# Decay sums of a state-space mixer as differences of running sums, formed on VectorE during the MLP

## The chip, the cores and the metric

One core of one Trainium2 chip runs the kernel. The metric is the device time of one execution in microseconds (us). Before the change it is 813.77 us, the median of three runs (813.22 to 813.79). All arithmetic is fp32; each fp32 matrix product shows as two MATMUL records in the trace.

## The reference

Four sequences of 512 tokens with 256 features pass a Mamba-2 style layer with an MLP, and then a mixture of 8 experts of which each token takes 2. Cut to what the change touches (h heads = 8, chunks of 128 tokens, state 128):

```python
dt = softplus(zxbcdt[..., -NHEADS:] + dt_bias)
xBC = silu(dw_causal_conv(xBC, conv_w, conv_b))      # x, B and C
A_cum = cumsum(dA, axis=-1)                          # dA = dt * A, within a chunk
L = exp(segsum(dA))                                  # exp(A_cum[l] - A_cum[s]) for s <= l, else 0
Y_diag = einsum('bcln,bcsn,bhcls,bcshp->bclhp', C, B, L, x * dt)
states = einsum('bcln,bhcl,bclhp->bchpn', B, exp(A_cum[-1] - A_cum), x * dt)
# the state is carried from chunk to chunk; Y_off = C @ state, scaled by exp(A_cum)
y = Y_diag + Y_off + D * x
y = rmsnorm(y * silu(z), mixer_norm_w)
h1 = res + y @ out_proj_w
out = h1 + silu(h2 @ gate_w) * (h2 @ up_w) @ down_w  # h2 = rmsnorm(h1)
```

## The kernel before

Every engine has an instruction list of its own, written out by hand; semaphores join them, and each engine takes its instructions strictly in that order. The list of each engine is a `body(b, prev, nxt)` for one sequence: sequence 0, a loop (two turns) over sequences 1 and 2, and sequence 3. `prev` adds the router's work for the sequence before, `nxt` the projections for the next one. SBUF is one tensor named `big`, PSUM one named `ps` with 8 banks of 512 columns, so rows of the trace name only these two and lines tell operations apart.

A body has two halves. The first is the scan over the four chunks c of 128 tokens. On TensorE: `seg_` (L434) multiplies a triangular matrix by the masked steps, which gives the sums of dA between any two tokens for all 8 heads (128x1024, banks 4 and 5); `front` (L358, L424) transposes x and B and forms the scores C.B; `yT_` transposes the gated y of the chunk before; `back` forms C.state (`off`, L446), the diagonal product of 8 heads (L451) and the chunk's own state (L459); `out_` (L476) is the output projection of the chunk before; `xnT_` and `logits` (L358, L494) are the router's product for the sequence before, one chunk at a time. On GpSimd: `masked_dA` (L1394) makes the masked steps, `scaled_x` (L1399) is x·dt, `plus_x_D` (L1404) adds D·x, `gated` (L1410) multiplies by silu(z), `scale_y` (L1361, L1415, L1417) turns the sum of squares into a scale. On VectorE: `front` (L1041, L1044) masks the scores and multiplies them into the decays, `off` (L1050, L1052), `y_` (L1059, L1062), `state` (L1067, L1071), `h1_` (L1082 to L1090), `decayed_x` (L1078), and `xn_` (L1099), the normalised rows of the sequence before. On ScalarE: `decay` (L787) is the Exp of the sums, then copies out of PSUM, D·x (L807) and the sum of squares of y (L829).

The second half holds dt (L374), the decays' small products (`dec_`, L382), the projections and the convolution of the next sequence (L391, L402, L1026), and the MLP (L547, L552, L566), whose end on TensorE is the end of the body. In it VectorE multiplies gate by up (L1255) and does the router's slots (L1149 to L1159), after which GpSimd scatters them. After the fourth sequence follow the tail of the routing and 39 expert tiles.

## Time and profile before

| | us |
|---|---|
| time, median of 3 runs | 813.77 |
| the profiled execution's own time | 808.96 |
| its span, first to last instruction | 807.1 |
| TensorE busy | 728.0 (90%) |
| VectorE busy | 577.3 (72%) |
| GpSimd busy | 307.4 (38%) |
| ScalarE busy | 227.4 (28%) |

The profiled execution is a single one, and its time lies 4.81 us below the median of the runs. In the rows further down PE is TensorE's matrix products, PEld its weight loads, DVE VectorE, ACT ScalarE, POOL GpSimd and SP the engine that issues the plain DMAs. "L434" is line 434 of the kernel before. The idle time in square brackets is what passed on that engine before the row, with the engine whose instruction ended it. A row of the order of time may hold several instructions of one line; its length is from the first start to the last end, so neighbouring rows overlap a little, and the time from start to start is what one costs the engine.

### The profile page before, as it was taken

Reading aid. Unit: us, or ns where it says so; the run is one execution under the profiler, and the core shown is the slowest. Engines: PE = TensorE matmul, PEld = TensorE weight load, DVE = VectorE, ACT = ScalarE, POOL = GpSimd, SP = SyncE. Lnnn points to the kernel's source line nnn. Section 1 sums busy time; section 2 is a strip of 40 time slices with the busy share of each in tenths; the row PEclk is TensorE's granted clock in tenths of the full one; section 3 lists DMA queues with packets and bytes.
Section 4 is the critical chain, followed back from the end, with each engine's and each line's share of the span. In section 5 each row is a group of like instructions: output and inputs, shape, how many; then the busy total and the mean of one; then the engine's idle time right before and its main releaser. Section 6 shows DMA issues by size and latency. Waiting matters only on the chain.

```text
span 807.1 us, 10348 instructions
## 1 busy us (share of the span) xinstructions
PE 728.0 (90%) x2751; PEld 464.5 (58%) x2752; DVE 577.3 (72%) x1370; ACT 227.4 (28%) x482; POOL 307.4 (38%) x505
## 2 busy tenths in 40 slices
PE   5888999899998999979608999999999999999992
PEld 3466547664667547655504666666666666666661
DVE  4686827868477865853634888888888888888870
ACT  1654544544444534631102111111111111111110
POOL 1266203740456315532242333344433344333422
PEclk9999999999999999999758999999999999999997
DMA  9800001000010000038617211111211112111111
GB/s 324 293 2 1 1 0 53 2 0 0 2 52 0 0 0 27 26 120 274 181 31 276 47 32 26 27 26 29 35 28 26 26 26 32 32 26 26 26 15 19
DMA packets 30167, 43.74 MB, mean 54 GB/s; under 512 B 4099, under 2 KB 23875, under 8 KB 30128
## 3 DMA queue, kind: packets, MB, share of 16 engines
q1 hardware_dynamic: 21600, 33.15, 12.3%
q0 software_dynamic: 8544, 10.30, 8.0%
q8 instruction: 12, 0.20, 0.1%
q14 instruction: 11, 0.09, 0.0%
HBM read 33.84 MB, written 9.75 MB: 54 GB/s over the span
## 4 chain that ended last, share of the span: by engine, by line
PE 64%; DVE 11%; issue 9%; POOL 9%; DMA 3%; ACT 2%; DVEq 0%; POOLq 0%; ACTq 0%; SPq 0%
PE ps L701 28%; PE ps L714 14%; PE ps L391 5%; PE ps L402 3%; PE ps L547 3%; PE ps L358 3%; PE ps L552 3%; POOL lists L1426 2%; POOL big L1404 2%; DVE big L1318 2%; PE ps L476 1%; DVE big L1026 1%; PE ps L566 1%; PE ps L434 1%; PE ps L374 1%
## 5 line engine op out<-in xcount | busy, mean ns | idle before, releaser
L1318 DVE STREAM_TRANSPOSE big<-big 32x224 f32<-32x224 f32 x608 | 244.8, 403 | 9.1
L701 PE MATMUL ps<-big 128*128 x624 | 242.7, 542 | 1.1 <-ACT big L932 1.1
L701 PEld LDWEIGHTS ps<-big 128*128 128x128 f32 x624 | 119.0, 191 | 106.1 <-issue 104.1
L1361 POOL TENSOR_TENSOR big<-big 128x1 f32<-128x1 f32 x179 | 56.6, 316 | 280.3 <-DVE big L1326 159.5
L714 PE MATMUL ps<-big 128*128 x546 | 124.5, 380 | 2.1 <-DVE big L1338 1.3
L714 PEld LDWEIGHTS ps<-big 128*128 128x128 f32 x546 | 100.8, 190 | 15.0 <-issue 2.9
L938 ACT ACTIVATE big<-ps 128x896 f32<-128x896 f32 x39 | 35.8, 917 | 217.2 <-PE ps L701 217.2
L358 PE MATMUL ps<-big 128*128 128x128 f32 (+1 forms) x327 | 52.3, 281 | 39.9 <-DMA big<-lists,big 16.0
L358 PEld LDWEIGHTS ps<-big 128*128 128x128 f32 (+1 forms) x327 | 39.8, 144 | 69.6 <-issue 28.6
L1333 DVE TENSOR_TENSOR big<-big,ps 128x896 f32<-128x896 f32 x39 | 42.4, 1087 | 47.5 <-PE ps L701 47.4
L1503 POOL DMA_INDIRECT out_rows<-big x39 | 63.3, 1623 | 23.8 <-issue 23.8
L1026 DVE SCALAR_TENSOR_TENSOR big<-ps,big 128x511 f32<-128x511 f32 (+2 forms) x72 | 52.9, 746 | 11.0 <-ACT big L778 9.4
L391 PE MATMUL ps<-big 128*128 128x512 f32 x96 | 47.6, 634 | 0.8 <-DVE big L1026 0.8
L932 ACT ACTIVATE big<-ps 128x256 f32<-128x256 f32 x39 | 14.9, 383 | 111.6 <-PE ps L358 111.6
L1426 POOL DMA_INDIRECT lists<-big x32 | 31.9, 997 | 37.9 <-DVE big L1159 28.6
L1492 POOL DMA_INDIRECT big<-xn_rows,big x39 | 40.2, 1030 | 5.9 <-issue 0.5
L566 PE MATMUL ps<-big 128*128 128x256 f32 x192 | 42.1, 379 | 0.0
L566 PEld LDWEIGHTS ps<-big 128*128 128x128 f32 x192 | 36.3, 190 | 5.2 <-issue 0.5
L547 PE MATMUL ps<-big 128*128 128x512 f32 x80 | 37.9, 596 | 1.0 <-DVE big L1245 1.0
L552 PE MATMUL ps<-big 128*128 128x512 f32 x80 | 37.6, 592 | 0.0
L451 PEld LDWEIGHTS ps<-big 128*128 128x128 f32 x256 | 31.4, 195 | 8.3 <-issue 6.3
L1399 POOL TENSOR_TENSOR big<-big 128x512 f32<-128x512 f32 x16 | 17.5, 1092 | 48.6 <-ACT big L795 48.6
(173 smaller groups left out, 924.4 us busy)
## 6 DMA issues: line engine op xcount, KB each, us to landing
big<-in_w SPq DMA_DIRECT2D x24, 896.0 KB, 11.8
out_rows<-big SPq DMA_DIRECT2D x4, 512.0 KB
xn_rows<-big SPq DMA_DIRECT2D x4, 512.0 KB
big<-in_hidden SPq DMA_DIRECT2D x1, 1536.0 KB, 11.8
big<-in_in_proj SPq DMA_DIRECT2D x1, 1288.0 KB, 6.9
big<-in_gate SPq DMA_DIRECT2D x1, 640.0 KB, 12.8
big<-in_up SPq DMA_DIRECT2D x1, 640.0 KB, 8.7
big<-in_down SPq DMA_DIRECT2D x1, 640.0 KB, 9.2
```

The lines of the kernel that those rows point to most:

```text
L358: return nc.tensor.transpose(out_ap, in_ap, ident[0:n, 0:n])
L391: last = mm(bank(4 + j % 2), win[:, k, INNER + j * P:INNER + (j + 1) * P], hT[:, k, :], start=(k == 0), stop=(k == KD - 1))
L547: last = mm(bank(bk), wgate[:, k, j * P:(j + 1) * P], h2T[:, k, :], start=(k == 0), stop=(k == KD - 1))
L552: last = mm(bank(bk + 1), wup[:, k, j * P:(j + 1) * P], h2T[:, k, :], start=(k == 0), stop=(k == KD - 1))
L566: last = mm(bank(t % 2)[:, 0:D], hid[:, j, t * P:(t + 1) * P], wdown[:, j, :], start=(j == 0), stop=(j == JB - 1))
L701: last = mm(bank(bk + n)[:, 0:HALF], xT[:, k, :], expert_cols(e, off + k * M + n * HALF, HALF), start=(k == 0), stop=(k == KD - 1))
L714: last = mm(bank(7)[:, 0:D], hTs[:, half, j * P:(j + 1) * P], expert_cols(e, 2 * KD * M + j * D, D), start=(j == 0), stop=(j == MB - 1))
L1026: last = V.scalar_tensor_tensor(xc[:, j, s:SEQ], bank(4 + j % 2)[:, 0:SEQ - s], vec[:, w:w + 1], xc[:, j, s:SEQ], ALU.mult, ALU.add)
L1318: last = V.transpose(hTs[c * SQ:(c + 1) * SQ, half, :].rearrange("p (j t) -> p j t", j=MB)[:, :, q * SQ:(q + 1) * SQ], ha[q * SQ:(q + 1) * ...
L1361: G.tensor_tensor(idle[:, k:k + 1], half[:, 0:1], half[:, 0:1], ALU.add)
L1426: G.indirect_dma_start(lists, bass.IndirectOffsetOnAxis(ap=slots[:, t, k:k + 1], axis=0), recs[:, t, k, :], None).then_inc(rec_out, 16)
L1503: G.indirect_dma_start(out, bass.IndirectOffsetOnAxis(ap=sidx, axis=0), ys, None, compute_op=ALU.add, bounds_check=TOKENS + P - 1, oob_is_ ...
```

## The change

The sums between two tokens are no longer a product on TensorE. `dec_` makes one more small product, the running sums of dA with the 32 pairs of chunk and head as rows; ScalarE copies it to SBUF (`cumT`), SyncE writes it to HBM (16 KB) and reads it back four times, each time 4 KB spread to all 128 partitions (`spread`), straight into `em`, which now has four chunks instead of two. VectorE subtracts the running sum of the row's own token and takes the minimum with 0 (`apart`, eight instructions of 128x128 for one chunk), ScalarE forms Exp in place (`decay`), VectorE multiplies by the masked scores (`scores`). For a next sequence all of this stands in the MLP: `apart` behind the first four gate-up products, `decay` behind the last gate activation, `scores` between the additions of the MLP's output. The first sequence has `apart` among its convolutions and the last three `scores` in its scan.

The transposes of B and the scores C.B of all chunks are formed at once during the MLP (`bg_`, banks 4 and 5) and masked in one instruction (`masked_G`). `decayed_x` moves from VectorE to GpSimd. The gate is distributed: GpSimd multiplies (off + D·x) by silu(z), VectorE multiplies the diagonal product out of PSUM by silu(z) (`yz`) and adds both. The transposed y has bank 5 instead of sharing bank 0 with the output projection. The router's transposes and logits are done in two halves of two chunks instead of four. `masked_dA` and `seg_` are gone.

```diff
+            def spread(n):
+
+
+                sp.wait_ge(cumT_taken, nth(n, 1, 0))
+                if not (isinstance(n, int) and n == 0):
+                    sp.wait_ge(y_ps, n * CH)
+                sp.dma_start(cum_rows, cumT[0:CH * HEADS, :]).then_inc(cum_out, 16)
+                sp.wait_ge(cum_out, nth(n, 16, 15))
+                for c in range(CH):
+                    sp.dma_start(em[:, c, :].unsqueeze(1),
+                                 cum_rows[c * HEADS:(c + 1) * HEADS, :].rearrange("(o h) l -> o (h l)", o=1).unsqueeze(0).to_broadcast([P, 1, HEADS * P])).then_inc(cum_in[c], 16)
...
+                if nxt:
+                    spread(b + 1)
...
+                mm(bank(1)[0:CH * HEADS, P:2 * P], dA.rearrange("p a b -> p (a b)"), tri_upto, start=True, stop=True).then_inc(dec_ps, 1)
...
-            seg_(0, 0, False)
+            bg_(0)
             front(0, 0, False)
 
             def body(b, prev, nxt):
                 for c in range(CH):
-                    if c + 1 < CH:
-                        seg_(b, c + 1, prev)
-                    if prev and c > 0:
-                        logits(b - 1, c - 1, b)
                     if c + 1 < CH:
                         front(b, c + 1, prev)
                     if c > 0:
                         yT_(b, c - 1)
-                    if prev and c > 0:
-                        xnT_(b - 1, c, b)
+                    if prev and c == 1:
+                        xnT_(b - 1, 0)
                     back(b, c, prev)
-                    if prev and c == 0:
-                        xnT_(b - 1, c, b)
+                    if prev and c == 2:
+                        logits(b - 1, 0)
+                        xnT_(b - 1, 1)
                     if c > 0:
                         out_(b, c - 1)
-                if prev:
-                    logits(b - 1, CH - 1, b)
+                    if prev and c == 3:
+                        logits(b - 1, 1)
                 if prev:
                     pe.wait_ge(lg_taken, b)
                 if nxt:
-                    pe.wait_ge(bg_taken, nth(b, CH, CH - 1))
+                    pe.wait_ge(xs_taken, nth(b, CH, CH - 1))
                     hT_(b + 1)
                 yT_(b, CH - 1)
                 if nxt:
                     pe.wait_ge(s_taken, nth(b, CH - 1, CH - 2))
                     dt_(b + 1)
-                    pe.wait_ge(seg_taken, nth(b, CH, CH - 1))
                     xbc_(b + 1, 0)
                 out_(b, CH - 1)
                 if nxt:
...
+                    if nxt and j == 1:
+                        bg_(b + 1)
                     if prev and j == 1:
                         positions(b - 1)
-                    if nxt and j == JB - 2:
-                        seg_(b + 1, 0, True)
...
+                A(cumT[0:CH * HEADS, :], bank(1)[0:CH * HEADS, P:2 * P], ACT.Copy).then_inc(cumT_taken, 1)
+                A(cums.rearrange("p a b -> p (a b)"), bank(1)[:, CH * HEADS:2 * CH * HEADS], ACT.Copy).then_inc(cums_taken, 1)
                 A(dec.rearrange("p a b c -> p (a b c)"), bank(1)[:, 0:3 * CH * HEADS], ACT.Exp).then_inc(dec_taken, 1)
...
             def decay(b, c):
-                act.wait_ge(seg_ps, nth(b, CH, c))
-                A(em[:, c % 2, :], bank(4, 2), ACT.Exp).then_inc(seg_taken, 1)
+                act.wait_ge(apart_ready, nth(b, CH, c))
+                A(em[:, c, :], em[:, c, :], ACT.Exp).then_inc(decays, 1)
...
-                        decay(b, c + 1)
                         front(b, c + 1)
                     if c >= 1:
                         yT_copy(b, c - 1)
-                    if prev:
-                        xnT_copy(b - 1, c)
+                    if prev and c in (1, 2):
+                        xnT_copy(b - 1, c - 1)
                     if c >= 1:
                         square_y(b, c - 1)
...
-                    if nxt and j == JB - 2:
-                        decay(b + 1, 0)
-                if nxt:
+                    if nxt and j == 2:
+                        bt_copy(b + 1)
+                if nxt:
+                    decay(b + 1, 0)
                     front(b + 1, 0)
+                    for c in range(1, CH):
+                        decay(b + 1, c)
...
+            def apart(n, c):
+
+
+                v.wait_ge(cums_taken, nth(n, 1, 0))
+                v.wait_ge(cum_in[c], nth(n, 16, 15))
+                for hh in range(HEADS):
+                    q = slice(hh * P, (hh + 1) * P)
+                    last = V.tensor_scalar(em[:, c, q], em[:, c, q], cums[:, c, hh:hh + 1], 0.0, ALU.subtract, ALU.min)
+                last.then_inc(apart_ready, 1)
+
+            def masked_G(n):
+                v.wait_ge(bg_ps, nth(n, 1, 0))
+                V.tensor_tensor(gm, bank(5).rearrange("p (c l) -> p c l", c=CH),
+                                tri_upto.unsqueeze(1).to_broadcast([P, CH, P]), ALU.mult).then_inc(gm_ready, 1)
+
+            def scores(b, c):
+                v.wait_ge(gm_ready, nth(b, 1, 0))
+                v.wait_ge(decays, nth(b, CH, c))
+                V.tensor_tensor(heads(em[:, c, :]), heads(em[:, c, :]),
+                                gm[:, c, :].unsqueeze(1).to_broadcast([P, HEADS, P]), ALU.mult).then_inc(em_ready, 1)
...
                 v.wait_ge(y_ps, nth(b, CH, c))
                 if c == 0:
-                    v.wait_ge(xsd_ready, nth(b, CH, c))
-                    V.tensor_tensor(yb[:, 0, :], xsd[:, 0, :], bank(6), ALU.add).then_inc(y_taken, 1)
-                else:
-                    v.wait_ge(y3_ready, nth(b, CH - 1, c - 1))
-                    V.tensor_tensor(yb[:, c % 2, :], yb[:, c % 2, :], bank(6), ALU.add).then_inc(y_taken, 1)
+                    v.wait_ge(z_taken, nth(b, CH, CH - 1))
+                if not (isinstance(b, int) and b == 0 and c == 0):
+                    v.wait_ge(y4_ready, b * CH + c)
+                V.tensor_tensor(yz, bank(6), sz[:, c, :], ALU.mult).then_inc(y_taken, 1)
+                v.wait_ge(y_taken, nth(b, CH, c))
+                v.wait_ge(y3_ready, nth(b, CH, c))
+                V.tensor_tensor(yb[:, c % 2, :], yb[:, c % 2, :], yz, ALU.add).then_inc(y4_ready, 1)
...
             def body(b, prev, nxt):
 
                 V.tensor_copy(cur_mv, mv)
                 V.tensor_copy(cur_rs, rs).then_inc(cur_kept, 1)
                 v.wait_ge(cur_kept, nth(b, 1, 0))
-                if prev:
-                    xn_(b - 1)
                 for c in range(CH):
-                    if c + 1 < CH:
-                        front(b, c + 1)
+                    if not prev and c + 1 < CH:
+                        scores(b, c + 1)
...
@@ -1216,8 +1245,8 @@
                     state(b, c)
                     if c > 0:
                         h1_(b, c - 1)
-                    if c + 1 < CH - 1:
-                        decayed_x(b, c + 1)
+                    if prev and c == 0:
+                        xn_(b - 1)
                     if nxt and c == 0:
                         ln1_stats(b + 1)
...
+                    if nxt and j < CH:
+                        apart(b + 1, j)
+                    if nxt and j == 2:
+                        masked_G(b + 1)
+                if nxt:
                     for t in range(CH):
+                        scores(b + 1, t)
                         add_mlp(b, t)
-                        if t == 1:
-                            decayed_x(b + 1, 0)
                     ln2_stats(b, ALL, CH)
...
-            def masked_dA(n, c):
-                g.wait_ge(dA_ready, nth(n, 1, 0))
-
-                if not (isinstance(n, int) and n == 0 and c < 2):
-                    g.wait_ge(seg_ps, n * CH + c - 1)
-                G.tensor_tensor(heads(mda[:, c % 2, :]), tri_upto.unsqueeze(1).to_broadcast([P, HEADS, P]),
-                                over_head(dA[:, c, :], P), ALU.mult).then_inc(mda_ready, 1)
...
             def gated(b, c):
-                g.wait_ge(y_taken, nth(b, CH, c))
                 if c == 0:
+                    g.wait_ge(xsd_ready, nth(b, CH, c))
                     g.wait_ge(z_taken, nth(b, CH, CH - 1))
-                G.tensor_tensor(yb[:, c % 2, :], yb[:, c % 2, :], sz[:, c, :], ALU.mult).then_inc(y4_ready, 1)
+                    G.tensor_tensor(yb[:, 0, :], xsd[:, 0, :], sz[:, 0, :], ALU.mult).then_inc(y3_ready, 1)
+                else:
+                    g.wait_ge(y2_ready, nth(b, CH - 1, c - 1))
+                    G.tensor_tensor(yb[:, c % 2, :], yb[:, c % 2, :], sz[:, c, :], ALU.mult).then_inc(y3_ready, 1)
...
-                    if c + 2 < CH:
-                        masked_dA(b, c + 2)
+                    if c == 0:
+                        gated(b, 0)
                     if c + 1 < CH:
                         scaled_x(b, c + 1)
+                    if c + 1 < CH - 1:
+                        decayed_x(b, c + 1)
                     if c > 0:
+                        scale_y(b, c - 1)
                         plus_x_D(b, c)
-                        scale_y(b, c - 1)
-                    gated(b, c)
+                        gated(b, c)
...
-                if nxt:
-                    masked_dA(b + 1, 0)
-                    masked_dA(b + 1, 1)
                 if prev:
                     scatter(b - 1)
                 if nxt:
                     scaled_x(b + 1, 0)
+                    decayed_x(b + 1, 0)
...
```

TensorE, chunk 2 of the loop's scan (line 358 are transposes, 446 to 459 the back of the chunk, 494 the logits, 476 the output projection of chunk 1), before:

```order
L428 REGISTER_ALU
L434 MATMUL ps<-big 128x512 x2
L491 REGISTER_ALU
L494 MATMUL ps<-big 128x8 x2
L358 MATMUL ps<-big 128x128 x5
L424 MATMUL ps<-big 128x128
L358 MATMUL ps<-big 128x128 x6
L446 MATMUL ps<-big 128x512
L451 MATMUL ps<-big 128x64 x8
L456 REGISTER_ALU
L459 MATMUL ps<-big 128x512
L476 MATMUL ps<-big 128x256 x4
```

and after (379 transposes, 460 to 475 the back, 510 logits, 492 output projection):

```order
L379 MATMUL ps<-big 128x128 x8
L460 MATMUL ps<-big 128x512
L465 MATMUL ps<-big 128x64 x8
L470 REGISTER_ALU
L475 MATMUL ps<-big 128x512
L506 ISA
L510 MATMUL ps<-big 128x8 x4
L379 MATMUL ps<-big 128x128 x4
L492 MATMUL ps<-big 128x256 x4
```

The product L434 is gone from the top, front's transposes and those of y follow each other directly (x8), and the router's transposes stand as four (L379 x4) behind the logits, which themselves stand behind the back of the chunk. Before, the router's two transposes stood ahead of the back, among the six.

On ScalarE the Exp and one copy of each chunk are gone; in chunk 2 the copy of the transposed xn (`xnT_copy`) keeps its place between the copy of the transposed y and the square of y.

GpSimd, chunk 2 of the same scan up to the gate (1399 scaled_x, 1404 plus_x_D, 1361 to 1417 scale_y, 1410 the gate), before:

```order
L1399 TENSOR_TENSOR big<-big 128x512
L1403 REGISTER_ALU
L1404 TENSOR_TENSOR big<-big 128x512
L1361 TENSOR_TENSOR big<-big 128x1
L1415 TENSOR_SCALAR big<-big 128x1
L1416 REGISTER_ALU
L1417 TENSOR_TENSOR big<-big 128x1
L1410 TENSOR_TENSOR big<-big 128x512
```

and after (1422 scaled_x, 1392 to 1450 scale_y, 1434 plus_x_D, 1443 the gate):

```order
L1422 TENSOR_TENSOR big<-big 128x512
L1392 TENSOR_TENSOR big<-big 128x1
L1448 TENSOR_SCALAR big<-big 128x1
L1449 REGISTER_ALU
L1450 TENSOR_TENSOR big<-big 128x1
L1433 REGISTER_ALU
L1434 TENSOR_TENSOR big<-big 128x512
L1443 TENSOR_TENSOR big<-big 128x512
```

scale_y of the chunk before now stands ahead of plus_x_D.

## Rows read from the trace of the kernel before

**Rows 1.** Stretch, its length, busy us of each engine (instructions), granted clock, DMA share, GB/s.

```profile
...
131.00:224.00 93.00, 87.86 (x368) 56.67 (x367) 64.50 (x158) 43.26 (x100) 40.88 (x47) 0.98 0.04 12
...
```

**Rows 2.** TensorE in order of time, loop turn 1: start, us, what, [idle before].

```profile
...
130.95 1.88 PE L434 MATMUL ps<-big 128*128 128x512 f32 x4
132.66 0.71 PE L358 MATMUL ps<-big 128*128 128x128 f32 x5
...
137.54 0.44 PE L358 MATMUL ps<-big 128*128 128x128 f32 x2 [1.29 <-DVE big L1099]
...
151.87 1.02 PE L446 MATMUL ps<-big 128*128 128x512 f32 x2
152.73 1.89 PE L451 MATMUL ps<-big 128*128 128x64 f32 x16
154.46 1.08 PE L459 MATMUL ps<-big 128*128 128x512 f32 x2
155.38 1.89 PE L476 MATMUL ps<-big 128*128 128x256 f32 x8
...
159.39 1.46 PE L358 MATMUL ps<-big 128*128 128x128 f32 x6 [1.78 <-DVE big L1087]
...
169.02 1.92 PE L374 MATMUL ps<-big 128*128 128x8 f32 x16 [0.50 <-DVE big L992]
...
176.04 0.75 PE L382 MATMUL ps<-big 128*128 128x32 f32 x6
...
213.48 10.53 PE L566 MATMUL ps<-big 128*128 128x256 f32 x48
...
```

**Rows 3.** The same for TensorE in the first and the last sequence.

```profile
...
76.92 1.92 PE L374 MATMUL ps<-big 128*128 128x8 f32 x16 [0.38 <-DVE big L992]
...
316.76 1.88 PE L434 MATMUL ps<-big 128*128 128x512 f32 x4
...
345.27 0.84 PE L358 MATMUL ps<-big 128*128 128x128 f32 x6 [2.21 <-DVE big L1087]
...
351.56 0.63 PE L358 MATMUL ps<-big 128*128 128x128 f32 x4 [0.72 <-POOL big L1410]
...
```

**Rows 4.** Groups by line, 131 to 169 us: busy us, mean ns of one, idle before.

```profile
...
L1410 POOL TENSOR_TENSOR big<-big 128x512 f32<-128x512 f32 x4 | 5.1, 1270 | 3.0 <-PE ps L434 3.0
L1404 POOL TENSOR_TENSOR big<-big 128x512 f32<-128x512 f32 x3 | 4.6, 1542 | 5.4 <-DVE big L1050 5.4
...
L1099 DVE TENSOR_SCALAR big<-big 128x256 f32 x4 | 3.4, 897 | 1.2 <-POOL big L1471 1.2
...
L1399 POOL TENSOR_TENSOR big<-big 128x512 f32<-128x512 f32 x3 | 3.2, 1054 | 0.0
...
L1050 DVE TENSOR_TENSOR big<-ps,big 128x512 f32<-128x512 f32 x3 | 2.1, 685 | 1.0 <-PE ps L446 1.0
...
L829 ACT ACTIVATE big<-big 128x512 f32<-128x512 f32 x3 | 1.9, 636 | 0.0
L1417 POOL TENSOR_TENSOR big<-big 128x1 f32<-128x1 f32 x3 | 1.8, 589 | 0.2
...
```

**Rows 5.** VectorE in order of time, first, third and last sequence.

```profile
...
42.42 2.80 DVE L1044 TENSOR_TENSOR big<-big 128x1024 f32<-128x1024 f32 x1
...
199.22 1.28 DVE L1255 TENSOR_TENSOR big<-big,ps 128x512 f32<-128x512 f32 x2
...
203.22 0.16 DVE L1149 TENSOR_TENSOR big<-ps,big 128x8 f32<-128x8 f32 x1
...
205.55 0.17 DVE L1159 CAST big<-big 128x8 int32<-128x8 f32 x1 [0.16 <-DVE big L1158]
...
357.65 1.14 DVE L1239 TENSOR_SCALAR big<-big 128x256 f32<-128x256 f32 x4 [1.75 <-POOL big L1461]
...
```

**Rows 6.** DMA issues of the page: count, size, us from issue to landing.

```profile
...
big<-in_hidden SPq DMA_DIRECT2D x1, 512.0 KB, 3.4
...
```

**Rows 7.** Stretches of 1.5 us in turn 2, columns as in rows 1.

```profile
...
262.00:263.50 1.50, 1.50 (x4) 0.98 (x5) 0.77 (x4) 0.69 (x3) 0.00 (x0) 0.50 0.00 0
263.50:265.00 1.50, 1.50 (x3) 0.47 (x3) 1.29 (x7) 0.28 (x2) 0.98 (x3) 0.50 0.00 0
...
```

149 lines of the change are left out of this document (74 added, 75 removed).

## The prediction

> **What bounds the kernel now.** I read the busy time by stretch first, then the order of time on TensorE through one sequence, then the groups by line for the price of one instruction, and last the other engines where TensorE waits. From 131 to 224 us, one turn of the loop over sequences, TensorE is busy 87.9 of 93.0 us, VectorE 64.5, GpSimd 40.9, ScalarE 43.3 [rows 1]. Behind the four sequences lies the expert part, which the change leaves alone. So each sequence is bounded by TensorE, except for short idle stretches in the scan over four chunks. I count times within a turn from S, the end of the previous MLP: 130.95 and 316.76 us [rows 2, 3]. The idle stretches end with VectorE's normalised rows (137.54) and with an h1 row (159.39) [rows 2]. The scan ends, for the rest of the sequence, when the dt product starts: S+38.07 (169.02) [rows 2]; in the first sequence at 76.92; in the last one the transposes of y for chunk 3 start at 351.56, S+34.8 [rows 3].
>
> **Removed from TensorE.** The product of the masked steps, L434: 132.66 - 130.95 = 1.71 us [rows 2], four per sequence, sixteen in all: 27.4 us. Added are a product of 32 by 128 (about 0.2 us beside the three of L382) and nothing else; the transposes of B and the scores C.B move from the four chunks into the MLP, 4 x 0.33 = 1.3 us. Three of the four L434 lie in the scan and one in the MLP. If TensorE stayed the bound, the whole 27.4 us less four times 0.2 would be won. It can only be won where nothing else is then late, so I followed the scan again with the durations of the rows.
>
> **The MLP stretch.** VectorE takes on, behind each of the first four gate-up products, eight TENSOR_SCALAR of 128x128, and once the mask (0.6). The trace has no such instruction of 128 columns. Nearest row: L1239, four of 256 columns with one per-partition scalar, 1.14 us, so (1.14 - 0.41)/3 = 0.24 us from start to start [rows 5]; half the columns can't cost more, and no less than half of it, 0.12. Near to neither end, I take the middle: 0.18, 1.45 us for eight. VectorE then runs, from the first hid product at 199.22: five hid products of 0.61, 2.5 for the routing slots (203.22 to 205.72), 0.6, four times 1.45 [rows 5]: it ends at about 211.5. TensorE's first down product, at 213.48 before [rows 2], would be due at 213.48 - 1.71 - 0.33 + 1.3 = 212.7. So it fits with 1.2 us to spare at 0.18, and ends 0.9 us late at 0.24. The Trainium skill ("VectorE: DVE Perf Modes", Mode 2×_2P) says that an fp32 tensor_scalar within SBUF takes two elements a cycle; the row agrees as far as it goes (256 columns in 0.24 us), and by the page alone the sum would be the same. ScalarE's Exp of the decays moves behind the last gate activation, its multiplications by G between the additions of the MLP's output; the down products (10.5 us from 213.48) hide both. The transfers: dec is at 176.04 [rows 2], the spread tiles are first read at 199.8, behind the first hid product. A 512 KB transfer took 3.4 us to land [rows 6]; a write of 16 KB and four of 512 KB would land 6 to 16 us after 177, so 0 on the path; even at double that only the first tile would be near. Gain of the MLP stretch with the missing L434 (1.71), less the 1.3 moved in, plus 0.33 that front no longer has, less 0.2: 0.5 us in each of three sequences.
>
> **The scan, sequences 1 and 2.** Prices: a GpSimd product of 128x512 1.25 (L1410), the first kind 1.05 (L1399), a VectorE one from PSUM 0.6 to the next and 0.69 to its end (L1050), GpSimd's three small ones of scale_y 1.1 with the power of 0.59 (L1417), ScalarE's square 0.64 (L829) and 0.2 to read its sum [rows 4].
> Chunk 0: GpSimd's power for the rows of the sequence before ends at S+2.8 as now, then it gates x·D (to 4.1). VectorE adds yz behind it, but its add has both inputs in SBUF and meets GpSimd's next product. In the trace such a product took 2.80 instead of 1.22 us with GpSimd at work [rows 5], and the four normalised rows 0.9 each instead of 0.35 [rows 4]; so I let each wait for GpSimd's end: add until 5.7, state copy 6.3, the four rows of xn, now behind them, until 8.7. TensorE, done with chunk 0 at S+3.5, transposes y at 5.8, then waits for xn until 8.8: chunk 1's off product starts at about S+9.3, before at S+11.07. The Trainium skill ("SBUF — State Buffer", Who interferes with whom) has the same as an exclusive lock of one port pair; the 2.80 us row agrees.
> Chunk 1: ScalarE copies the transposed xn first and has the sum of squares at 10.8; GpSimd's scale_y now stands ahead of plus_x_D: 12.0, 13.2, and gating 14.5; VectorE adds to 15.3, state 15.9; off(2) at S+16.0. Before S+20.9 (151.87). TensorE had 0.86 + 1.73 + 0.92 + 1.72 of work [rows 2], so 0.45 us idle only.
> Chunk 2: here a new wait stands. ScalarE's copy of the second half of xnT comes ahead of the square of y(1), and TensorE makes that half only behind all of back(2) and the logits: 16.0 + 3.5 + 0.75 + 0.45 = 20.7. So the copy ends at 21.4, the square at 22.2; GpSimd 1.1 + 1.25 + 1.25 to 25.9; VectorE's add 26.7. TensorE finishes out(1) at 22.4 and idles 4.3 us; off(3) at S+27.4. Before S+29.7.
> Chunk 3: VectorE has h1(1), h of the next sequence, off(3) until 30.5; GpSimd 31.9 and 33.1; add 33.9; then h1(2) 1.3 and hT1 0.75: dt at S+36.1 against 38.07. Gain 2.0. What went missing: 5.1 us of L434 and 4 us of idle time were to be had, and the chain y(c) to off(c+1) by way of VectorE, GpSimd twice, VectorE (6 to 6.5 us) and the detour in chunk 2 took the rest. The chain is longer than before by the gate product, since the state is now behind the add that waits for it.
>
> **Sequence 0** has no xn, but GpSimd's decays and ScalarE's Exp of the fourth tile stand ahead of x·D: first product of y at about 44 (45.2 before, where VectorE's product ended [rows 5]), off(1) at 52 to 53, dt 76.6 against 76.92: 0.3. **Sequence 3**: no work for a next one; y(3) is transposed at S+33.2 against 34.8: 1.6.
>
> **The sum.** 0.3 + 2 x 2.0 + 1.6 in the scans, 3 x 0.5 in the MLPs: 7.4 us. Against it stands TensorE's clock. At 159.39, behind 1.78 us idle, six transposes took 1.46 us, at 345.27, behind 2.21 us idle, the same six 0.84 [rows 2, 3]. From 262 to 265 us TensorE was granted 0.50, the level of 1.2 GHz [rows 7]; such a stretch of 3 us costs half of itself, 1.5 us, where TensorE is the bound. The change makes idle stretches of 4.3 us. I take one more such stretch, with what is left of it at its edges 1.7 us, in the whole kernel. 5.7 us remain. The profiled execution took 808.96 us (span 807.1), which is 4.8 below the median of 813.77; the difference is made within the execution and taken off the median: 808.1 us.
>
> **Rivals.**
> A. TensorE stays the bound: the collisions and the detour of chunk 2 cost little, for instance since ScalarE's order matters less than I think. For it: TensorE busy 94% of a turn. Against it: orders fixed in the code, above all the copy ahead of the square. With 4.3 us back in three sequences and half of the other losses it is 813.8 - 5.7 - 13 - 3 = 792; all of it, 787. Chance 0.08.
> B. Half of it: VectorE and GpSimd don't block each other in chunk 0 and 1 (1.0 to 1.5 us each) as I let them. L1099 may have run partly between GpSimd's products. 808.1 - 3 x 2.3 = 801. Chance 0.17.
> C. Slower by the clock: each of the three later sequences idles at S+4, S+7 and S+23. If in all four sequences two stretches at 1.2 GHz fall into work that bounds (hT, dt and xbc behind the scan), that is 8 x 1.5 = 12 us against the two stretches, 3 us, of now: 9 more on the 7.4 gained, 815.4; with the eight at 0.24 us each (0.9 in two sequences) 817.2. It decides from five such stretches more than before. The Trainium skill ("TensorE: Matmul & The Clock Gate", What's actually happening) has the clock throttled by default and released by activity; the trace shows both, a drop after 1.8 us and none after 2.2. Chance 0.13.
> D. No change to be measured: seven collisions of 1 us more than I counted. 813.8. Chance 0.09.
> The forecast as it stands: 0.53, with its own range of 804 to 812.
>
> **How the numbers follow.** A measurement of this kernel tells 0.2% from no change, 1.6 us: faster is below 812.1, slower above 815.4. Faster: A, B and nearly all of the forecast's 0.53, 0.77; same: D, a part of C and the forecast's edge, 0.12; slower 0.11. The range of 8 in 10 leaves out A and the upper part of C: 799 to 815.
>
> **What would show it.** Right: no L434; TensorE idle about 4 us ahead of the y transposes of chunk 3 with a release that leads back to GpSimd and ScalarE's square; xn as releaser at S+8.8; dt at S+36; no wait in the MLP; the spread landed by 195. Wrong: turns of under 88 us (A), an idle TensorE ahead of the first down product (the eight dearer than 0.22 us each), or the granted clock under 0.96 in all turns (C).

## The result, and the profile after

The changed kernel took 835.76 us (median of 4; 828.51 to 838.68) against 813.78 (813.22 to 814.22) for the kernel before, run beside it: a ratio of 1.0246, 95% interval 1.0213 to 1.028. It is slower by 22 us, where 5.7 us less was forecast. The profiled execution took 838.68 us with a span of 836.9. Its page, busy time and the granted clock in 40 slices:

```profile
span 836.9 us, 10346 instructions
...
PE 742.4 (89%) x2695; PEld 482.3 (58%) x2696; DVE 584.1 (70%) x1490; ACT 219.2 (26%) x466; POOL 292.6 (35%) x501
...
PEclk9957999779998799789965999999999999999997
```

TensorE has 56 instructions fewer than before (2751) and yet 14.4 us more busy time (728.0 before). Work has got dearer by the clock: the last line falls to 5, 7 or 8 in slices 3 and 4, 8 and 9, 13 and 14, 17 and 18, once per scan. (The 6 and 5 in slices 21 and 22, behind the routing's tail, have their like in the kernel before, whose line reads 7, 5, 8 in slices 20 to 22.)

TensorE in order of time through one turn of the loop (start, us, what, [idle before]); the turn's S is 140.22:

```profile
140.22 0.60 PE L379 MATMUL ps<-big 128*128 128x128 f32 x4
140.90 2.00 PE L465 MATMUL ps<-big 128*128 128x64 f32 x16
...
145.90 0.65 PE L379 MATMUL ps<-big 128*128 128x128 f32 x4 [1.65 <-DVE big L1095]
149.44 1.12 PE L379 MATMUL ps<-big 128*128 128x128 f32 x4 [2.89 <-DVE big L1125]
150.35 1.91 PE L460 MATMUL ps<-big 128*128 128x512 f32 x2
152.06 3.51 PE L465 MATMUL ps<-big 128*128 128x64 f32 x16
...
171.34 0.66 PE L379 MATMUL ps<-big 128*128 128x128 f32 x4 [4.11 <-DVE big L1095]
172.02 1.71 PE L460 MATMUL ps<-big 128*128 128x512 f32 x2
173.52 3.52 PE L465 MATMUL ps<-big 128*128 128x64 f32 x16
176.83 3.12 PE L492 MATMUL ps<-big 128*128 128x256 f32 x8
...
183.13 1.92 PE L395 MATMUL ps<-big 128*128 128x8 f32 x16 [0.50 <-DVE big L1010]
```

The three waits are those of the prediction: 1.65 us for y(0), xn as releaser (L1125) ahead of chunk 1, and 4.11 us ahead of the transposes of y for chunk 3. What stands behind them isn't: the sixteen products of y take 3.51 us instead of 1.89 [rows 2], the output product 3.12 instead of 1.89. The dt product starts at S+42.9, against S+38.07 before [rows 2] and S+36.1 forecast. In windows (columns as in rows 1) the two stretches behind the waits, and the worst one, in the first sequence:

```profile
148.00:158.00 10.00, 8.56 (x26) 6.35 (x27) 6.50 (x17) 3.11 (x11) 6.34 (x10) 0.52 0.16 54
172.00:179.00 7.00, 6.98 (x23) 5.73 (x24) 4.71 (x11) 1.60 (x5) 4.07 (x7) 0.53 0.00 0
...
42.00:63.00 21.00, 17.93 (x65) 13.03 (x64) 16.63 (x40) 13.83 (x36) 13.66 (x13) 0.52 0.32 116
```

A granted clock of 0.50 is the 1.2 GHz level. Up to 390 us such stretches add up to some 100 us here and to some 13 before.

These two profiled executions lie on opposite sides of their kernels. The one of the kernel before has a granted clock of 0.965 and 808.96 us, where its other executions on record have 0.952 to 0.967 and 811 to 820 us; the one of the changed kernel is the slowest of its four. Their spans differ by 29.8 us, the medians by 22. A second trace of the kernel before, with only its loop written out (e9 below, 817.74 us), has some 30 us at the low level up to 390 us instead of 13. So the turns below overstate what the change cost, 29.8 us where the medians give 22; against e9 the clock added 6 us in a turn instead of 8.

To weigh clock against waits I cut every kernel from one first product of y to the next, a whole turn. In that window the busy time less the length times (1 - clock) is the work at the full clock; the product itself is what the clock added (a little too much, as idle time is counted in). The clock has two digits, so a term is good to half a us. The same turn, before and after:

```profile
133.43:226.33 92.90, 87.76 (x368) 56.57 (x367) 64.51 (x158) 43.26 (x101) 40.88 (x48) 0.98 0.04 11
...
45.28:133.43 88.15, 84.14 (x338) 53.23 (x339) 57.43 (x120) 40.21 (x91) 29.58 (x37) 0.98 0.01 4
```

```profile
140.90:240.14 99.24, 89.19 (x353) 59.26 (x353) 67.70 (x189) 40.90 (x96) 37.35 (x46) 0.90 0.09 33
...
46.62:140.90 94.28, 90.32 (x324) 58.98 (x324) 63.10 (x150) 41.96 (x101) 30.04 (x37) 0.84 0.08 30
```

Before: 85.9 work, 1.9 clock, 5.1 idle. After: 79.3 work, 9.9 clock, 10.05 idle. So 6.6 us of work went, as the four L434 say; 4.9 us of waits came, as I had counted; and 8 us of clock came, which I had not. In the first sequence (the second line of each pair) the turn is 6.1 us longer with no more idle time than before (3.96 against 4.01 us): 7.1 us less work and 13.3 us of clock, 0.84 where it was 0.98. The four sequences give 6.1, 6.3, 6.0 and, with everything behind the last, 10 us, and the start 1.3: together the 29.8 us between the two spans. The expert tiles have no part in it: from their first transposes (451.74 us here, 421.69 before) to the end they take 385.2 and 385.4 us.

In the table of the experiments, three of e1's ten executions and two of e16's nine lay over 1.5% above the fastest of their kernel, the profiled ones among them; their medians and ratios are of the others, and their turns aren't given.

One more thing stands in the second turn of the loop. VectorE, first instruction behind the jump back:

```profile
241.00 0.17 DVE L1204 TENSOR_SCALAR big<-big 128x4 f32<-128x4 f32 x1
245.65 1.02 DVE L1233 COPY big<-big 128x8 f32<-128x8 f32 x1 [4.48 <-issue]
```

It waits for no other engine, only for its own issue, and TensorE then waits 5.03 us for VectorE's add, where the turn before has 1.65. That I had not seen coming. Not all of the 3.4 us more is lost, since xn is then ready sooner (0.78 us of waiting instead of 2.89): the off product of chunk 1 starts at S+12.3 instead of S+10.1. The same copy behind the jump in the kernel before:

```profile
225.91 0.17 DVE L1202 COPY big<-big 128x8 f32<-128x8 f32 x1 [0.36 <-issue]
```

### The profile page after: what moved, and what is told of

It is laid out like the page before. It is cut to its first block, busy times and chain, and to the rows that moved or that the text cites. A ratio compares the mean times of both kernels' runs of the same rounds, so it can differ in the third digit from the quotient of the medians.

```text
span 836.9 us, 10346 instructions
## 1 busy us (share of the span) xinstructions
PE 742.4 (89%) x2695; PEld 482.3 (58%) x2696; DVE 584.1 (70%) x1490; ACT 219.2 (26%) x466; POOL 292.6 (35%) x501
## 4 chain that ended last, share of the span: by engine, by line
PE 72%; issue 10%; DVE 8%; POOL 4%; DMA 3%; ACT 2%; DVEq 0%; POOLq 0%; SPq 0%
PE ps L710 27%; PE ps L723 13%; PE ps L412 5%; PE ps L492 4%; PE ps L379 4%; PE ps L465 3%; PE ps L563 3%; PE ps L568 3%; PE ps L582 2%; PE ps L423 2%; PE ps L460 2%; DVE big L1349 1%; PE ps L395 1%; DVE big L1125 1%; DMA lists<-big 1%
## 5 line engine op out<-in xcount | busy, mean ns | idle before, releaser
L710 PEld LDWEIGHTS ps<-big 128*128 128x128 f32 x624 | 119.1, 191 | 105.9 <-issue 104.0
L379 PE MATMUL ps<-big 128*128 128x128 f32 (+1 forms) x327 | 59.1, 301 | 57.4 <-DVE big L1095 23.6
L723 PEld LDWEIGHTS ps<-big 128*128 128x128 f32 x546 | 100.8, 190 | 14.9 <-issue 2.9
L379 PEld LDWEIGHTS ps<-big 128*128 128x128 f32 (+1 forms) x327 | 44.3, 155 | 88.1 <-issue 26.8
L465 PEld LDWEIGHTS ps<-big 128*128 128x128 f32 x256 | 45.2, 266 | 13.0 <-issue 11.2
L412 PE MATMUL ps<-big 128*128 128x512 f32 x96 | 49.0, 649 | 0.4 <-DVE big L1044 0.4
L1422 POOL TENSOR_TENSOR big<-big 128x512 f32<-128x512 f32 x16 | 19.2, 1201 | 77.2 <-ACT big L806 77.1
L465 PE MATMUL ps<-big 128*128 128x64 f32 x256 | 44.3, 348 | 1.9 <-DVE big L1191 1.1
L492 PE MATMUL ps<-big 128*128 128x256 f32 x128 | 42.0, 486 | 0.7 <-ACT big L830 0.7
L582 PE MATMUL ps<-big 128*128 128x256 f32 x192 | 42.1, 379 | 0.0
L492 PEld LDWEIGHTS ps<-big 128*128 128x128 f32 x128 | 32.6, 261 | 13.3 <-issue 7.0
## 6 DMA issues: line engine op xcount, KB each, us to landing
big<-in_gate SPq DMA_DIRECT2D x1, 640.0 KB, 13.3
```

Source lines behind the costliest of these rows:

```text
L379: return nc.tensor.transpose(out_ap, in_ap, ident[0:n, 0:n])
L412: last = mm(bank(4 + j % 2), win[:, k, INNER + j * P:INNER + (j + 1) * P], hT[:, k, :], start=(k == 0), stop=(k == KD - 1))
L465: last = mm(bank(6)[:, hh * HD:(hh + 1) * HD], em[:, c, hh * P:(hh + 1) * P], xdt[:, c % 2, hh * HD:(hh + 1) * HD], start=True, stop=True)
L492: last = mm(bank(0)[:, 0:D], yTs[:, k, :], wout[:, k, :], start=(k == 0), stop=(k == 3))
L582: last = mm(bank(t % 2)[:, 0:D], hid[:, j, t * P:(t + 1) * P], wdown[:, j, :], start=(j == 0), stop=(j == JB - 1))
L710: last = mm(bank(bk + n)[:, 0:HALF], xT[:, k, :], expert_cols(e, off + k * M + n * HALF, HALF), start=(k == 0), stop=(k == KD - 1))
```

## The experiments

The theory: TensorE lost work that lay between the waits of the scan, so that these waits, which come as forecast, let the clock fall, and the work behind each wait ran at half the clock. Rivals: the waits alone carry the loss; or the jump does. Ratios are to the kernel before, run beside each group. "Turn" is the turn of the loop as above, in the profiled execution; "w / c / i" its work, clock and idle us. Only the first of the loop's two turns is given; the second can differ by several us (changed 98.92, e2 98.93, e5 102.02, e7 90.69, e12 89.0). A fill is one product of `keep_warm(bank, n)`, which both kernels have: n products of the identity with 128x256 constants, which nobody reads.

| kernel | median us | ratio (95%) | turn | w / c / i |
|---|---|---|---|---|
| changed | 835.76 | 1.0246 (1.0213-1.028) | 99.24 | 79.3 / 9.9 / 10.1 |
| e1_square_first | 812.34 | 0.9946 (0.9914-0.9979) | | |
| e2_fill_seg | 825.95 | 1.0104 (1.0075-1.0133) | 93.77 | 83.9 / 4.7 / 5.2 |
| e3_no_seg | 811.7 | 0.9936 (0.9912-0.9959) | 93.07 | 79.2 / 6.5 / 7.4 |
| e4_router_later | 809.29 | 0.9912 (0.9877-0.9947) | 89.39 | 79.0 / 3.6 / 6.9 |
| e5_fill_waits | 831.31 | 1.0153 (1.0116-1.019) | 96.20 | 87.0 / 3.8 / 5.3 |
| e6_unrolled | 833.97 | 1.0213 (1.0175-1.0251) | 94.58 | 79.9 / 4.7 / 9.9 |
| e7_later_fill | 804.4 | 0.9841 (0.9811-0.9871) | 87.11 | 85.9 / 0 / 1.3 |
| e8_later_fill_unrolled | 797.05 | 0.9764 (0.9732-0.9795) | 87.02 | 85.8 / 0 / 1.2 |
| e9_before_unrolled | 817.21 | 1.0004 (0.9983-1.0025) | 94.37 | 85.6 / 3.8 / 5.0 |
| e10_later_unrolled | 808.23 | 0.9903 (0.9868-0.9937) | 89.52 | 79.2 / 3.6 / 6.7 |
| e11_stats_later_fill | 794.12 | 0.9719 (0.969-0.9747) | 85.67 | 84.8 / 0 / 0.9 |
| e12_stats_later | 805.28 | 0.9857 (0.9813-0.9902) | 87.19 | 80.0 / 1.7 / 5.4 |
| e13_before_fill | 818.46 | 1.0038 (1.0019-1.0058) | 92.95 | 90.1 / 0 / 2.8 |
| e14_after_fill_unrolled | 825.27 | 1.0132 (1.0097-1.0166) | 96.08 | 87.0 / 3.8 / 5.2 |
| e15_no_seg_fill | 819.13 | 1.0049 (1.0027-1.0071) | 93.98 | 85.8 / 3.8 / 4.5 |
| e16_no_seg_fit | 809.33 | 0.9931 (0.9902-0.9961) | | |
| e17_after_fit_unrolled | 814.2 | 1.0012 (0.9989-1.0034) | 93.41 | 87.8 / 1.9 / 3.7 |
| e18_stats_later_fit | 795.74 | 0.9765 (0.9736-0.9794) | 87.19 | 83.5 / 1.7 / 2.0 |

**Work taken away, work put in.** Two edits of opposite sense. In the kernel before, the decay sums' product alone is cut to 8 columns (the decays are then not computed):

```
-                for i in range(2):
-                    last = mm(bank(4 + i), tri_after, mda[:, c % 2, i * 512:(i + 1) * 512], start=True, stop=True)
-                last.then_inc(seg_ps, 1)
+                mm(bank(4)[:, 0:8], tri_after, mda[:, c % 2, 0:8], start=True, stop=True).then_inc(seg_ps, 1)
```

> The kernel before with the product L434 cut to 8 columns; so the decays are not computed, everything else and every wait stays. Saves up to 16 x 1.6 = 26 us of TensorE. Clock theory: thinner work alone lowers the granted clock in the scan below that of before; 800 to 812. Wait theory: TensorE was the bound, so 790 to 797, with the granted clock at 0.96.

It was 0.6% faster, 5 us, for 26 us of work taken out. Its turn is no shorter than before (92.90 us there, 94.37 in e9):

```profile
134.80:227.87 93.07, 85.68 (x360) 58.03 (x359) 64.64 (x159) 43.42 (x101) 40.75 (x47) 0.93 0.04 12
```

6.7 us of work went; 2.3 us of idle time and 4.6 of clock took its place. The granted clock, mean of the executions, is 0.936 against 0.957 for the kernel before beside it. The 811.7 us lie at the edge of the clock theory's 800 to 812 and far from the waits' 790 to 797. The new transfers can't be what lowers the clock either: this kernel has none of them. But less work and longer waits came together here, so the run doesn't tell which of the two lowers it. In the changed kernel, useless products were put where L434 had stood, ahead of each chunk of the scan:

```
                 for c in range(CH):
                     if c + 1 < CH:
+                        keep_warm(3, 4)
+                    if c + 1 < CH:
                         front(b, c + 1, prev)
```

> The changed kernel with useless products of TensorE in the places of the removed ones in the scan: four of 128x256 (1.7 us at full clock, the length of L434) at the head of chunks 0 to 2, twelve times in all, into a bank that nobody reads. Clock theory: 20.6 us of work are added and yet the time falls or stays, 815 to 832, since the stretches at 1.2 GHz get shorter or go. Wait theory: the fillers lie in front of work that bounds, or in idle time at best: 836 to 850.

20.6 us of work more made it 10 us faster than the changed kernel, within the expected range. If waits were all, fills could at best be free.

**The order around the waits.** ScalarE's square of y ahead of its copy of xnT:

```
-                    if prev and c in (1, 2):
-                        xnT_copy(b - 1, c - 1)
                     if c >= 1:
                         square_y(b, c - 1)
+                    if prev and c in (1, 2):
+                        xnT_copy(b - 1, c - 1)
```

> The changed kernel (835.8 us), with ScalarE's copy of the transposed xn behind the square of y instead of ahead of it in chunks 1 and 2. The idle stretch of 4.1 us ahead of y's transposes in chunk 3 should go from three sequences. Clock theory (the waits let TensorE's granted clock fall for 7 to 10 us, and that is where the loss lies): 836 - 12 of idle time - some 7 of half-speed work = about 817, with the stretch at 1.2 GHz behind chunk 3's start gone. Wait theory (the waits themselves are the loss, the clock comes along): 836 - 12 = 824 and the granted clock where it was, 0.92.

Two lines give 3% back, some 24 us, more than either expectation. The detour of chunk 2 was real. It had cost waits of 4.11 us in three sequences, 12.3 us, so about as much again came back otherwise, and the granted clock rose from 0.917 to 0.925 in the changed kernel's executions to 0.925 to 0.936 here. Executions of this one program also part by the clock: at 0.936 and 0.933 they took 807.93 and 807.45 us, at 0.926 and 0.925 818.07 and 815.27. Next, TensorE's transposes of xn behind the products of chunk 1, too:

```
-                    if prev and c == 1:
-                        xnT_(b - 1, 0)
                     back(b, c, prev)
+                    if prev and c == 1:
+                        xnT_(b - 1, 0)
```

> The changed kernel with the router's first transposes behind the back of chunk 1 instead of ahead of it, and ScalarE's copies of them behind the square of y. Takes both long idle stretches away (2.9 us in chunk 1 on xn, 4.1 in chunk 3), 21 us in three sequences. Clock theory: also the stretches at 1.2 GHz behind them, 836 - 21 - 15 = about 800. Wait theory: 836 - 21 = 815.

809.29 us lies between what the two theories expected (about 800 and 815). The turn fell to 89.39 us; the first sequence, which has no router part, kept its low stretch from 41 to 61 us.

**Useless work in the waits.** Here I first made two mistakes, which the expectations carry: one 128x256 fill is two instructions and takes 0.43 to 0.47 us, not 0.24; and in e5 and e14 six stood ahead of y(1), where that order has no wait, with two ahead of y(2), where it waits 4.11 us.

```
+            keep_warm(3, 5)
             bg_(0)
@@
                     if c > 0:
+                        keep_warm(3, (4, 6, 2)[c - 1])
                         yT_(b, c - 1)
                     if prev and c == 1:
+                        keep_warm(3, 4)
                         xnT_(b - 1, 0)
@@
+                    keep_warm(1, 3)
                     dt_(b + 1)
```

> The changed kernel with useless 128x256 matmuls of the identity (0.24 us each at the full clock, 0.43 to 0.47 at half) put only where TensorE waits anyway: 5 ahead of the first sequence's C.B products, 4 ahead of the turning of y(0), 4 ahead of xn's transposes, 6 ahead of the turning of y(1), 2 ahead of that of y(2), 3 ahead of the dt product. About 5 us of new work per sequence, against waits of 1.65, 2.89, 4.11 and 1.4 us in the second sequence of the changed kernel. Theory 1 (the clock carries most of the loss: some 100 us of the layer part lie in stretches at 0.50, and work inside those is paid twice): the stretches at 0.50 shrink to under 50 us, the time falls by 12 to 20 us, to 816 to 824. Rival (the waits carry the loss and the low clock is only what they look like): the fills hide in waits or lengthen them, 836 to 842, and the waits keep their places.

It gained some 7 us, half of what was expected, and lies between the ranges of both theories. In the turn shown 7.7 us of fills bought 4.7 of idle time and 6.1 of clock; the second turn got 3.1 us longer, and of the rest the first sequence gave most: its turn took 89.45 us instead of 94.28. The same fills in the order of e4 (there y(1) does wait 2.9 us, and xn no longer does, so its four are left out):

> The version with the router's transposes behind the attention-like product and ScalarE's square ahead of its copy (809.3 us in the last runs), with the same useless matmuls (without the 4 ahead of xn's transposes, which no longer wait). Its stretches at 0.50 are some 78 us up to 392 us. Theory 1: the 20 us at half clock in the first sequence (41 to 62) and two thirds of the others go, time 796 to 803, under both kernels. Rival (waits): 809 to 813.

0.7% faster, 804 us, just above the expected range. With the loop written out as well:

```
-            with eng.Fori(1, SEQS - 1) as b:
+            for b in range(1, SEQS - 1):
                 body(b, True, True)
```

> The version of the run before this one with the loop over the middle sequences written out: if the jump is what holds VectorE up for 5.97 us and TensorE for 6.25 us at 238.36, it takes another 4 to 6 us off, 791 to 799; if not, the two are the same within 1 us.

797.05 us, within the expected 791 to 799. The turn, with a clock of 1.00:

```profile
133.38:220.40 87.02, 85.84 (x382) 58.07 (x382) 67.40 (x189) 40.93 (x96) 37.09 (x45) 1.00 0.11 37
```

e10 is the same without fills, the fourth corner of the square:

> Router's transposes later and the loop written out, without any useless matmuls. With the three runs e4_router_later, e7_later_fill and e8_later_fill_unrolled this makes a square of two edits. Theory (the fills give 5 us or more wherever TensorE waits, whether or not the loop is written out): this takes about 5 us off e4, ratio 0.984 to 0.988, which is 6 to 9 us above e8's ratio of 0.976. Rival (with the jump's stall gone the fills are worth nothing): ratio 0.975 to 0.978.

```profile
135.46:224.98 89.52, 82.78 (x353) 54.27 (x353) 67.48 (x189) 40.81 (x96) 37.13 (x45) 0.96 0.11 36
```

The fills' 6.6 us took 5.5 of idle time and 3.6 of clock; over the kernel 11 us were won by adding some 30 instructions a turn that compute nothing, more than the 6 to 9 expected. (The ratio of e10 itself, 0.9903, lies above both expected ranges: the loop alone gave next to nothing.) The rest of the square shows how the two edits need each other: written out alone the loop brought 0.1% (within the intervals), with fills 0.8%.

The controls. The kernel before, with fills in its own waits (0 to 4 at each), computes the same products:

```
                 if c > 0:
                     pe.wait_ge(o_taken, nth(b, CH, c - 1))
+                if c in (1, 2):
+                    keep_warm(0, (2, 4)[c - 1])
                 pe.wait_ge(y4_ready, nth(b, CH, c))
```

> The kernel before with useless 128x256 matmuls where it waits: 4 ahead of the first sequence's first decay sums, 4 ahead of its first y product (waits of 1.59 and 1.77 us there), and in each sequence 3 ahead of xn's first transposes (1.29), 2 and 4 ahead of the turning of y(1) and y(2) (0.89, 1.78). Clock theory: only some 13 us of its layer part lie at 0.50, so there is little to win: ratio 0.993 to 1.001. Rival (the fills act on something that both kernels have, so they explain nothing of the change): ratio under 0.99, as in the changed kernel's variants (0.9903 to 0.9764 there).

A little slower, outside the expected range on the upper side. The granted clock, mean of the executions, rose only from 0.957 to 0.963: with little time at the low level there is little to win, and the fills cost more than that. And fills in the same places, some more of them, for the kernel without the decay sums' products:

> As e3_no_seg (the kernel before, decay sums' products cut to 8 columns, so the decays aren't computed; ratio 0.9936) with useless matmuls in the waits: 4 ahead of the first decay sums, 5 ahead of the first y product of the first sequence, and in each sequence 6 ahead of xn's first transposes (2.84 us wait), 4 and 4 ahead of the turning of y(1) and y(2) (1.57, 1.78). Of the 26 us removed some 3.3 us per sequence are work again, but inside waits. Clock theory: the 61 us at 0.50 of e3 shrink to under 25, and the time falls by 8 to 14 us, ratio 0.976 to 0.984. Rival (the removal was worth only 4 us because the waits took its place, the clock is a side effect): ratio 0.992 to 0.998.

This failed: 1.0049 where 0.976 to 0.984 was expected. The clock did come back (0.936 to 0.958, mean of the executions), but 6.6 us of fills bought 2.9 of idle time and 2.7 of clock, since those ahead of y stand behind the wait for o_taken and so outlast what is left of the wait. Cut to 6, 1 and 1 (same edit, with 3 ahead of the first sums, and 4 ahead of the first y product, not 5 as the expectation says):

> As e15_no_seg_fill (decay sums' products cut to 8 columns, so the decays aren't computed), with fills cut to what fits in the waits: 3 ahead of the first sums, 5 ahead of the first y product of the first sequence, 6 ahead of xn (2.6 us in a wait of 2.84), 1 and 1 ahead of the turning of y(1) and y(2) (0.43 us each; 4 each before). e15's turn of 93.98 us was 85.7 us of work at the full clock, 3.8 of clock and 4.45 idle. Clock theory: idle 4.5 stays or rises to 5.5, fills fall from 6.6 to 3.5 us, the clock stays at 0.96 or better: turn of 90.5 to 92, ratio 0.980 to 0.990. Rival (a low clock costs nothing that the waits don't cost): as e3_no_seg, turn 92.5 to 93.5, ratio 0.992 to 0.996.

0.9931, the same as without fills, so the rival's number, though the clock did come back here too (0.936 in e3, 0.957 here, mean of the executions). In this kernel the fills cost what the clock gave. A part of it is their place: in e15's second turn those ahead of y(1) stand behind 2.27 us of another wait, on the path. The rest isn't explained, and e15 and e16 leave open what the removal alone would be worth at the full clock. Fills of the right size and place in the changed kernel's own order, loop written out, are the cleanest case; first the order with all its mis-placed fills:

> The changed kernel, order as it was, with the fills of e5_fill_waits and the loop written out. Alone they gave ratios of 1.0153 and 1.0213 against the changed kernel's 1.0246. Theory (clock, and the stall of 4.5 to 5.6 us at the jump, which with its low stretch behind it undid what the fills had won): together more than the sum of both, ratio 0.995 to 1.005. Rival (the waits for xn and y(1), 2.89 and 4.11 us, are themselves the loss): about the sum of both, ratio 1.010 to 1.015.

1.0132: about the sum of both edits, again the rival's number. Against this kernel:

```
-                        keep_warm(3, (4, 6, 2)[c - 1])
+                        keep_warm(3, (3, 0, 8)[c - 1])
@@
-                        keep_warm(3, 4)
+                        keep_warm(3, 6)
                         xnT_(b - 1, 0)
@@
-                    keep_warm(1, 3)
+                    keep_warm(1, 1)
```

> The changed kernel in its own order, loop written out, with fills in the waits it has and of their size: 3 ahead of the turning of y(0) (1.3 us, wait 1.61), 6 ahead of xn (2.6, wait 2.89), none ahead of y(1), 8 ahead of y(2) (3.5, wait 4.12), 1 ahead of dt. e6_unrolled's second turn was 79.9 us of work at the full clock, 4.7 of clock and 9.9 idle: 94.6. Clock theory: the fills take 7.8 us of the 9.9 idle and the 4.7 of clock go: turn of 90 to 91.5, ratio 0.998 to 1.006. Rival (waits alone): 94 to 95, ratio 1.015 to 1.022.

1.0012, in the expected range, against 1.0213 for e6 with the same order, the same waits and no fills: 16 us for nothing but useless work inside waits, with the granted clock at 0.957 instead of 0.917 (mean of the executions) and all of the change's transfers in place. The turn shown, 93.41 us, missed the expected 90 to 91.5 by 2, since 1.9 us of clock and 3.7 of idle time were left; the next one took 91.85. Its window and, from TensorE's order of time, the stretch behind the longest wait:

```profile
134.25:227.66 93.41, 89.69 (x388) 59.71 (x388) 67.42 (x189) 40.90 (x96) 36.97 (x45) 0.98 0.09 35
...
156.96 3.62 PE L590 MATMUL ps<-big 128*128 128x256 f32 x16
161.25 0.66 PE L379 MATMUL ps<-big 128*128 128x128 f32 x4 [0.67 <-DVE big L1099]
161.94 1.10 PE L460 MATMUL ps<-big 128*128 128x512 f32 x2
162.87 1.89 PE L465 MATMUL ps<-big 128*128 128x64 f32 x16
164.60 1.95 PE L492 MATMUL ps<-big 128*128 128x256 f32 x8
```

The wait of 4.11 us is filled but for 0.67, and the products of y behind it take 1.89 us, where the changed kernel took 3.52.

**The jump.** The changed kernel with the loop written out, nothing else:

> The changed kernel with the loop over the two middle sequences written out (same instructions, no jump back). In the changed kernel VectorE stands 4.48 us put down to issue in front of its first instruction behind the jump (245.65, L1233), and TensorE waits 5.03 us for it at 248.51, against 1.65 us at the same place one turn earlier; in the kernel before the same place shows 0.36 us. Theory (the jump back is paid by the fetch of the loop's first instructions, and the change moved VectorE's slack from there): that wait falls to the 1.65 us of the other turn, 3.4 us less and some 2 more by the clock, 829 to 833. Rival (the instructions are late for another reason, as GpSimd's or the queues'): 835 to 838, with the 4 to 5 us still there; longer code could also bring other waits of this kind.

```profile
234.57 0.16 DVE L1233 COPY big<-big 128x8 f32<-128x8 f32 x1
234.64 0.16 DVE L1234 COPY big<-big 128x4 f32<-128x4 f32 x1
237.22 0.69 DVE L1092 TENSOR_TENSOR big<-ps,big 128x512 f32<-128x512 f32 x1 [2.42 <-issue]
```

The wait at the copies is gone; 2.42 us stand at the next instruction instead, but TensorE's wait is back at 1.72 us (5.03). The whole is 0.3% less, within the intervals of the two and just above the expected 833. These traces also show what the clock alone costs, without any fills: in e6's first turn, ahead of any jump, TensorE is idle for 9.94 us, against 10.05 in the changed kernel, in the same places, and yet the turn is 4.7 us shorter, at 0.95 instead of 0.90. (It is the fastest of e6's four executions beside the slowest of the changed kernel's, so this is no gain of writing the loop out.)

```profile
139.05:233.63 94.58, 84.64 (x353) 56.27 (x353) 67.81 (x189) 40.90 (x96) 36.93 (x45) 0.95 0.10 34
```

> The kernel before the change with the loop over the two middle sequences written out. Theory (the jump back costs only where VectorE's chain has no slack at the head of the turn): here VectorE stands 0.36 us at the jump in the kernel before and one stall of 3.99 us put down to issue lies in the MLP, where TensorE didn't wait for it, so nothing is won: ratio 0.998 to 1.002. Rival (the loop costs in both kernels, so writing it out is no fair part of a comparison): 2 us or more faster, ratio under 0.9975.

No difference, as expected: with 0.36 us at that copy there was no stall of this kind to lose.

**The best version.** e10 with VectorE's statistics of the next sequence behind the scaling of off(1):

```
                     if c > 0:
                         off(b, c)
+                    if nxt and c == 1:
+                        ln1_stats(b + 1)
                     y_(b, c)
@@
-                    if nxt and c == 0:
-                        ln1_stats(b + 1)
```

> As e10_later_unrolled with the statistics behind off(1): no fills at all. TensorE's longest wait of a turn (2.90 us for y(1)) should fall to about 1 us. Clock theory: one of the low stretches per turn (153 to 158) starts behind that wait; it goes too, so the gain over e10 is 2 us per turn from the wait and 1 to 2 more from the clock: 6 to 10 us in all, ratio 0.974 to 0.979. Rival (only the waits count): 4 to 6 us.

3 to 4 us less, under both expectations, with intervals that overlap. The waits fell as they should (1.53 instead of 2.89 us ahead of y(1)), but the next turn took 89.0 us at 0.94: part of what a shorter wait gave, the clock took. The mean clock of the executions is 0.937 in both, so here a wait was paid once, not twice. With fills (4, 4, 2 ahead of y, 9 more in the first sequence):

> e8 with VectorE's statistics of the next sequence (L991 to L998, 1.9 us) behind the scaling of off(1) instead of ahead of it, so that GpSimd's two steps for y(1) start 1.9 us sooner; 4 instead of 6 fills ahead of the turning of y(1), and in the first sequence 9 more ahead of the first y product, where e8 still ran 7 us at the clock of 0.50 behind waits of 1.36 and 1.25 us. Theory: per turn 0.5 us (two fills) to 1.9 us less, first sequence 1.5 to 3 us less: ratio 0.966 to 0.973. Rival (fills set the time now, the wait only moves): 0.975 to 0.978.

```profile
134.92:220.59 85.67, 84.81 (x379) 57.24 (x379) 68.34 (x189) 40.89 (x96) 37.44 (x45) 1.00 0.12 38
```

794.12 us, 2.8% under the kernel before and 5% under the changed one, within the expected range. With five fills fewer per turn:

> e11_stats_later_fill with 3, 3 and 0 fills ahead of the turning of y(0), y(1), y(2) instead of 4, 4, 2 and 2 instead of 3 ahead of dt. e11's middle turns were 84.8 us busy, of which about 5.6 were fills, at a clock of 1.00, 0.9 idle. Five fills less are 2.1 us per turn: if the clock stays at 1.00 the turn is 83.6 to 85 and the ratio 0.965 to 0.971; if one low stretch comes back, 85.5 to 87 and ratio 0.972 to 0.978.

A low stretch came back in the turn shown (clock 0.98, 87.19 us), as the second case expected, and the ratio rose to 0.9765 (the intervals touch). In the next turn the clock stayed at 1.00, and it took 85.55 us where e11's took 85.69. So taking fills out of a turn with none of its clock lost wins next to nothing.

## Why the prediction was wrong

- **What is removed** was right: 6.6 us of TensorE's work per turn are gone.
- **The MLP stretch** was right: no wait ahead of the first down product. Eight subtractions from one hid product to the next:

```profile
215.49 0.69 DVE L1284 TENSOR_TENSOR big<-big,ps 128x512 f32<-128x512 f32 x1
216.09 1.65 DVE L1064 TENSOR_SCALAR big<-big 128x128 f32<-128x128 f32 x8
217.66 0.68 DVE L1284 TENSOR_TENSOR big<-big,ps 128x512 f32<-128x512 f32 x1
```

This is 1.57 us, so 0.20 each, between the bounds of 0.12 and 0.24. The spread tiles, issued from 194.91 us on, landed in 5.4 us, long before their use at 216. The forecast's own terms add up to 211.2 us and not to 211.5, so it had 1.5 us to spare at 0.18 and was 0.4 late at 0.24; nothing hangs on it.
- **The scan by hand** was right in what waits for what and nearly so in length: idle 1.65, 2.89 and 4.11 us, where I had let TensorE wait for y(0), for xn and 4.3 us for y. The transposes of xn started at S+9.2 (8.8), and from off(2) at 160.54 to off(3) at 172.02 it was 11.5 us (11.4). The add met GpSimd's product and took 1.45 us, and L1125 3.02 for its four; one turn later, where VectorE was late and GpSimd idle from 247.8 to 252.8 us, they took 0.69 and 1.38. So the collisions that rivals A and B doubted were real:

```profile
146.37 3.02 DVE L1125 TENSOR_SCALAR big<-big 128x256 f32 x4
...
248.97 1.38 DVE L1125 TENSOR_SCALAR big<-big 128x256 f32 x4
```

What came late is what stands behind the waits: off(2) at S+20.3 instead of 16.0, and dt 11.1 us behind off(3) instead of 8.7. 150.35 to about 159 and 172 to 179 is work at half the clock, forecast at the full one. In the same way dt of the first sequence came at 84.76 instead of 76.6 us, though its first product of y was only 2.6 us late (46.62), and y(3) of the last one was transposed at S+41.2 instead of 33.2.
- **The clock term failed**: "I take one more such stretch, with what is left of it at its edges 1.7 us, in the whole kernel." There are three per sequence, of 3 to 20 us, and against the kernel before they added 8 us in each turn, 13 in the first sequence and 10 in the last, with the routing's tail. So the term of 1.7 us for the whole kernel measured some 39 in this pair of executions. I had priced a stretch from two windows of the kernel before [rows 7], where it ended after 3 to 4 us, and took its length over to a kernel whose scan has less work and more waits.
- **Rival C** had the right mechanism and chance 0.13, and its sign, a granted clock under 0.96 in all turns, came (0.84, 0.90, 0.90). But it has the same size error: two stretches of 3 us per sequence gave 815.4 to 817.2, and 835.76 was measured. It also put them behind the scan, and the longest stand in it, right behind the waits. Rivals A and B fell with the waits, which were as counted. In e1 a wait was paid about twice, once as idle time and once as clock.
- **The jump back** was no term at all: 3.4 us more of waiting for y(0) in one turn, 2.2 us by the off product behind it.

The range ended at 815 since I let the clock vary in the number of stretches and not in their length.
